# Moving convolution taps and softplus sums of a Mamba stage to GpSimd, and z's gate off it

## The reference, cut to what matters

```
xz = h @ W_in;  xm, z = split(xz, 2)
xm = silu(depthwise_conv4(xm) + conv_b)
dtr, Bm, Cm = split(xm @ W_xp, [64, 80])
dt = softplus(dtr @ W_dt + b_dt)
for each step t:  h = h * exp(dt_t * A) + (dt_t * x_t) * B_t
                  y_t = sum over states of h * C_t
y = (y + xm * D_param) * silu(z)
out = y @ W_out
```

## Time and profile before

| what | value |
|---|---|
| median of three runs | 2338.74 us |
| the profiled execution: its time, its span | 2343.22 us, 2341.5 us |
| busy: TensorE, VectorE, ScalarE, GpSimd | 2053.8, 2057.8, 1682.8, 1345.3 us |
| mean granted TensorE clock | 0.968 of full speed |
| scan from its first to its last bank product | 610.49 to 2273.23 us |

### The profile page before, as it was taken

One profiled execution on the slowest core, in us unless ns is written; L12 is line 12 of the kernel. 1 busy time (PEld: TensorE's weight loads), 2 busy tenths in 40 slices (PEclk: granted clock), 3 DMA queues, 4 the chain that ended last, 5 costly groups with the idle time before them and its releaser, 6 DMA issues. The chain is left out here.

```text
span 2341.5 us, 44346 instructions
## 1 busy us (share of the span) xinstructions
PE 2053.8 (88%) x13497; PEld 1578.5 (67%) x13497; DVE 2057.8 (88%) x3846; ACT 1682.8 (72%) x3652; POOL 1345.3 (57%) x1544
## 2 busy tenths in 40 slices
PE   4899999995799999999999999999999999989870
PEld 3566666662576767777777768777776768777760
DVE  2788888884599999999999999999999999999983
ACT  1455555553788979888888879888887879888840
POOL 2799999984455646455455646455455646454530
PEclk8999999996799999999999999999999999999995
DMA  5122222211000000000000000000000000000218
GB/s 142 39 64 64 64 64 64 62 47 34 10 6 14 6 14 15 6 15 6 19 6 14 6 15 15 6 15 5 20 6 15 5 15 15 6 6 6 90 73 287
DMA packets 71470, 80.75 MB, mean 34 GB/s; under 512 B 12227, under 2 KB 63619, under 8 KB 69188
## 3 DMA queue, kind: packets, MB, share of 16 engines
q1 hardware_dynamic: 66052, 69.52, 9.2%
q10 hardware_dynamic: 5184, 8.39, 1.0%
HBM read 44.33 MB, written 33.55 MB: 33 GB/s over the span
## 5 line engine op out<-in xcount | busy, mean ns | idle before, releaser
L599 ACT ACTIVATE decay<-dtT,decay_rate 128x256 f32<-128x256 f32 x2048 | 869.4, 495 | 0.2
L495 PE MATMUL bank<-ident,decay 128*128 128x128 f32 x4096 | 623.0, 275 | 114.1 <-DVE fresh L715 39.4
L505 PEld LDWEIGHTS bank<-ident,scaled 128*128 128x128 f32 x4096 | 485.5, 142 | 233.2 <-issue 201.9
L505 PE MATMUL bank<-ident,scaled 128*128 128x128 f32 x4096 | 623.7, 275 | 2.1 <-POOL scaled L446 2.0
L495 PEld LDWEIGHTS bank<-ident,decay 128*128 128x128 f32 x4096 | 470.9, 141 | 159.4 <-ACT decay L599 127.1
L446 POOL TENSOR_SCALAR scaled<-state,bc 128x512 f32<-128x512 f32 x384 | 276.8, 728 | 432.0 <-DVE state L715 402.7
L446 POOL TENSOR_SCALAR scaled<-fresh,bc 128x512 f32<-128x512 f32 x384 | 283.8, 747 | 317.8 <-DVE fresh L715 260.6
L705 DVE TENSOR_TENSOR bank<-bank,fresh 128x512 f32<-128x512 f32 x512 | 338.7, 689 | 58.2 <-PE bank L495 56.2
L705 DVE TENSOR_TENSOR bank<-bank,state 128x512 f32<-128x512 f32 x512 | 334.6, 688 | 28.6 <-PE bank L495 22.9
L715 DVE SCALAR_TENSOR_TENSOR state<-dtx,bc,bank 128x512 f32<-128x512 f32 x512 | 356.5, 736 | 0.0
L715 DVE SCALAR_TENSOR_TENSOR fresh<-dtx,bc,bank 128x512 f32<-128x512 f32 x512 | 356.4, 735 | 0.0
(11 more groups left out here) (137 smaller groups left out, 3427.7 us busy)
## 6 DMA issues: line engine op xcount, KB each, us to landing
xt<-in_x_dram SPq DMA_DIRECT2D x64, 128.0 KB, 2.2
resid<-x SPq DMA_DIRECT2D x64, 128.0 KB, 1.8
normed<-xh SPq DMA_DIRECT2D x64, 128.0 KB, 1.7
xg<-normed SPq DMA_DIRECT2D x64, 128.0 KB, 2.1
ssm_out<-yo SPq DMA_DIRECT2D x32, 256.0 KB, 2.0
fin_r<-resid SPq DMA_DIRECT2D x8, 1024.0 KB, 13.1
mask_bc<-in_mask_BxS_ik_dram SPq DMA_DIRECT2D x64, 64.0 KB, 2.9
fin_y<-ssm_out SPq DMA_DIRECT2D x32, 128.0 KB, 3.0
```

What stands on the lines that cost most here:

```text
L495: mm = pe.transpose(dec_bank[i % DECAY_BANKS][:, m * P:(m + 1) * P], decay[:, i // BLOCK % 2, n % GROUP, m, t % HALF * P:(t % HALF + 1) * ...
L505: mm = pe.matmul(y_bank[t % HALF][:, m * P:(m + 1) * P], scaled[:, i % RING, m * P:(m + 1) * P], ident[:, :], is_transpose=True, start=Fal ...
L599: act.activation(decay[:, block % 2, e // CB, m, :], dtT[par][:, m, half * HTOK:(half + 1) * HTOK], ACT.Exp, scale=decay_rate[:, m, n:n + ...
```

## The change

Four parts move.

1. The taps of blocks 0 and 1 go to GpSimd. Each tap is there two instructions: a product of `raw` with the tap into the new tile `tap`, and a sum of `tap` into `xs` (`add_tap`, items 6 to 17, one instruction an item). VectorE keeps the six taps of blocks 2 and 3 (items 10 to 16). The blocks are gated in the order 0, 2, 3, 1 (`X_ORDER`), tanh at items 13, 16, 18, 20 and gate at items 15, 17, 19, 21.
2. The softplus sum goes to GpSimd: for each block a sum and then the product with x, eight instructions at items 39 to 46 (`softplus_times_x`). ScalarE's first dt instruction becomes Relu in place of Identity, so that the sum has no maximum in it.
3. z is no longer copied: ScalarE takes its tanh straight from the bank, and VectorE makes (tanh + 1) * z with z read from the bank (items 17, 18, 22, 30), which also frees the bank. The tanh over all of z and GpSimd's eight gate instructions go.
4. The order of the jobs: z3 stands between dt0 and dt1, at items 28 and 29; z2 moves to 20 and 21; dt1 to dt3 stand at 31, 33, 35, bc at 36 to 39, x0 to x3 at 49, 51, 53, 55. dtr takes the blocks in the order of `X_ORDER`.

Waits follow: ScalarE's absolute value of dt waits for all four gated blocks (`tmp` is used for both), the carry copy waits for both kinds of taps, VectorE's first y gate waits for the four z banks, and the last prefetch of the sync engine waits for x3 of chunk 14 in place of z.

```diff
-        JOBS = ("h0 h1 u0 u1 u2 u3 out1 z0 z1 z2 z3 "
-                "dtr dt0 dt1 dt2 dt3 bc out0 x0 x1 x2 x3").split()
+        JOBS = ("h0 h1 u0 u1 u2 u3 out1 z0 z1 z2 "
+                "dtr dt0 z3 dt1 dt2 dt3 bc out0 x0 x1 x2 x3").split()
...
-                                (14, 15), (16, 17), (18, 19), (20, 21),
-                                (22, 23, 24, 25), (27,), (29,), (31,), (33,), (35, 36, 37, 38),
-                                (42, 43, 44), (46,), (48,), (50,), (52,))))
...
+                                (14, 15), (16, 17), (20, 21),
+                                (22, 23, 24, 25), (27,), (28, 29), (31,), (33,), (35,), (36, 37, 38, 39),
+                                (42, 43, 44), (49,), (51,), (53,), (55,))))
+        POOL_TAPS = [(m, k) for m in (0, 1) for k in range(TAPS - 1)]
+        POOL_TAP_SLOT = 6
+        VECTOR_TAPS = {10: (2, 0), 12: (2, 1), 14: (2, 2), 13: (3, 0), 15: (3, 1), 16: (3, 2)}
+        X_ORDER, X_TANH, X_GATE = (0, 2, 3, 1), (13, 16, 18, 20), (15, 17, 19, 21)
+        Z_GATE = (17, 18, 22, 30)
+        MODULATE, CARRY, SOFTPLUS = (28, 33), 24, 39
...
+            def add_tap(c, par, at, step):
+                m, k = POOL_TAPS[at]
+                done = (c + 1) * len(POOL_TAPS) + at
+                x = xs[1 - par][:, m, :]
+                if step == 0:
+                    if k == 0:
+                        gp.wait_ge(s_tap0, (c + 1) * CB + m + 1)
+                    reached(gp, s_tapadd, done)
+                    apart(gp)
+                    gp.tensor_scalar(tap[:, :], raw[:, m, k * P:k * P + TOK], taps[:, m, k:k + 1], 1.0,
+                                     ALU.mult, ALU.mult).then_inc(s_tapmul, 1)
+                else:
+                    gp.wait_ge(s_tapmul, done + 1)
+                    gp.tensor_tensor(x, x, tap[:, :], ALU.add).then_inc(s_tapadd, 1)
+            def softplus_times_x(c, par, m, step):
+                v = dtT[1 - par][:, m, :]
+                if step == 0:
+                    gp.wait_ge(s_softexp, (c + 2) * (CB + 1))
+                    gp.tensor_tensor(v, v, tmp[:, m, :], ALU.add).then_inc(s_dt, 1)
+                else:
+                    gp.wait_ge(s_dt, (c + 1) * CB + m + 1)
+                    gp.tensor_tensor(tmp[:, m, :], v, xs[1 - par][:, m, :], ALU.mult).then_inc(s_dtxT, 1)
...
-                    ins = act.activation(zs[1 - par][:, k, :], side[:, :], ACT.Copy)
+                    act.activation(zs[1 - par][:, k, :], side[:, :], ACT.Tanh, scale=0.5).then_inc(s_ztanh, 1)
+                    return
...
+                            ve.scalar_tensor_tensor(z, z, 1.0, side_bank[b][:, :], ALU.add, ALU.mult)\
+                                .then_inc(s_side_moved[b], 1)
```

More of the change, by code:

```diff
@@ L161, in build @@
         bc = sb("bc", [P, 2, T, 2 * DS], ssm_mem)
+        tap = sb("tap", [P, TOK], ssm_mem)
         decay = sb("decay", [P, 2, GROUP, CB, HTOK], ssm_mem)
@@ L244, in build @@
         s_gated = sem("y_gated")
-        s_zmul = sem("z_times_tanh")
         s_yo = sem("y_rows_ready")
@@ L451, in body @@
                         scale_state(c, par, i)
+                    if pre and 0 <= i - POOL_TAP_SLOT < 2 * len(POOL_TAPS):
+                        add_tap(c, par, (i - POOL_TAP_SLOT) // 2, (i - POOL_TAP_SLOT) % 2)
                     if pre and i in MODULATE and c + 2 < CHUNKS:
@@ L459, in body @@
                             .then_inc(s_carried, 1)
[L460 to L476, removed]
+                    if pre and SOFTPLUS <= i < SOFTPLUS + 2 * CB:
+                        softplus_times_x(c, par, (i - SOFTPLUS) // 2, (i - SOFTPLUS) % 2)
             modulate(0, 0)
@@ L620, in move @@
                 elif kind == "dt":
-                    act.activation(dtT[1 - par][:, k, :], side[:, :], ACT.Identity, bias=dt_bias[:, k:k + 1])
-                    act.wait_ge(s_xs, (c + 1) * CB + k + 1)
+                    act.activation(dtT[1 - par][:, k, :], side[:, :], ACT.Relu, bias=dt_bias[:, k:k + 1])
+                    act.wait_ge(s_xs, (c + 2) * CB)
                     ins = act.activation(tmp[:, k, :], side[:, :], ACT.Abs, bias=dt_bias[:, k:k + 1])
@@ L658, in body @@
                             move(c, par, job)
[L659 to L663, removed]
+                    if pre and i in X_TANH:
+                        m = X_ORDER[X_TANH.index(i)]
+                        last = (m, TAPS - 2)
+                        if last in POOL_TAPS:
+                            act.wait_ge(s_tapadd, (c + 1) * len(POOL_TAPS) + POOL_TAPS.index(last) + 1)
+                        else:
+                            act.wait_ge(s_tap, (c + 1) * len(VECTOR_TAP_ORDER) + VECTOR_TAP_ORDER.index(last) + 1)
                         act.activation(tmp[:, m, :], xs[1 - par][:, m, :], ACT.Tanh, scale=0.5).then_inc(s_xtanh, 1)
@@ L720, in gate @@
                 if t == 0:
-                    ve.wait_ge(s_zs, (c + 1) * CB)
+                    for k in range(CB):
+                        moved(ve, c - 1, f"z{k}")
                 ve.wait_ge(s_summed, c * ITEMS + index_of(DS - 1, t) + 1)
@@ L762, in body @@
                                                     ALU.mult, ALU.add).then_inc(s_tap, 1)
[L763 to L774 removed]
+                        if pre and s in Z_GATE:
+                            k = Z_GATE.index(s)
+                            ve.wait_ge(s_ztanh, (c + 1) * CB + k + 1)
+                            b = side_turn(c, f"z{k}")[0]
+                            z = zs[1 - par][:, k, :]
+                            ve.scalar_tensor_tensor(z, z, 1.0, side_bank[b][:, :], ALU.add, ALU.mult)\
+                                .then_inc(s_side_moved[b], 1)
+                        if pre and s in X_GATE:
+                            m = X_ORDER[X_GATE.index(s)]
+                            ve.wait_ge(s_xtanh, (c + 1) * CB + X_GATE.index(s) + 1)
+                            ve.scalar_tensor_tensor(xs[1 - par][:, m, :], tmp[:, m, :], 1.0, xs[1 - par][:, m, :],
+                                                    ALU.add, ALU.mult).then_inc(s_xs, 1)
             mamba_bodies(ve, body)
```

37 lines of the change are left out of this document (14 added, 23 removed).

## The result

| | before | after |
|---|---|---|
| median, four runs each | 2338.91 us | 2361.61 us (2360.53 to 2364.41) |
| profiled execution: time, span | 2343.22, 2341.5 | 2364.41, 2362.7 |
| one chunk of the scan, most of them | 105.15 | 105.52 |
| end of the state's clearing to the scan's first item | 52.97 | 61.74 |

After to before is 1.0079, with a 95% interval of [1.0065, 1.0094]: 0.8% slower, which is small but clear of the noise. The forecast was 2350, range 2325 to 2370.

What follows compares the result with a forecast made beforehand. VectorE, TensorE and ScalarE were taken to bound different stretches of a chunk. 15 x (0.05 + 0.55) + 2.5 = 11.5 on the profiled 2343.2 gave 2354.7; with the median 4.5 lower, 2350 us, range 2325 to 2370.

Steps and rivals of the forecast that it cites:

- meetings: Items 8 to 20: VectorE instructions with two SBUF operands slowed beside GpSimd's, 2.37 us a chunk in all.
- Item 8 to item 20: VectorE's time over these items of a chunk, pairs, taps, gates, output rows and waits summed: 27.85 us.
- Item 22's transpose: TensorE's transpose issued at item 22: saved taps eaten by waits and z gates, so 0.05 us later.
- the large meeting: Item 14: VectorE's second tap held behind GpSimd's sum of block 1, 1.10 us.
- z3's copy was ahead of the chain ... Item 43's transpose comes 0.55 later: Items 22 to 48: z3's tanh lengthens ScalarE's dt and decay chain, delaying TensorE's transpose 0.55 us a chunk.
- Softplus: nothing gained, nothing lost in the loop: Before item 43: taking the 2.61 us sum off VectorE gains nothing, since item 43 waits for its transpose anyway.
- Sum +2.5 (0 to +6): Body(-1), where nothing hides anything: its delays and savings together add 2.5 us, bounds 0 to 6.
- block 1's sum and dtr: Body(-1): block 1's tap sum on GpSimd is ready about 1.3 us later.
- A: Rival: VectorE is the bound throughout, a chunk saves 4.8 us, 2269 us in all; chance 0.05.
- D: Rival: two more meetings with a sum, +2.0 us a chunk, 2380 us in all; chance 0.13.
- B: Rival: GpSimd and VectorE phases miss each other, item 22 is 1.0 to 1.6 us earlier, 2326 us; chance 0.22.
- C: Rival: no change, since z3's tanh finds a gap in ScalarE's work, 2342 us; chance 0.23.

Runs made afterwards that it cites:

- e4: Changed kernel without GpSimd's twelve tap instructions: 2341.32 us, 0.9986 of the kernel before; chunk 104.50 us.
- e1: Kernel before with only the taps of blocks 0 and 1 moved to GpSimd and the new block order: 2335.15 us, 0.9955 of the kernel before.
- e2: Kernel before with only the z part and the new job order, taps and softplus left on VectorE: 2383.49 us, 1.016 of the kernel before.
- e5: Changed kernel without ScalarE's tanh of z3, all products and bank waits kept: 2361.91 us, 1.0077 of the kernel before.
- e9: Changed kernel with z3's product moved behind dt3, to items 34 and 35: 2358.03 us, 1.0067 of the kernel before.
- e6: Changed kernel with the old places of z2, z3, dt1 to dt3 and bc: 2356.2 us, 1.0055 of the kernel before.
- e3: Kernel before with only the softplus sum moved to GpSimd, Relu for Identity and later x jobs: 2344.45 us, 0.9999 of the kernel before.
- e11: Kernel before with taps of blocks 0 and 1 on GpSimd except in body(-1), and out0 at items 54, 57, 60: 2289.84 us, 0.9773.
- e7: Changed kernel with all of body(-1)'s taps on VectorE: 2362.04 us, 1.0081 of the kernel before.

## Why the prediction was right, and where it was not

The direction and the reason for it were right: VectorE gave up 62.7 us (I had said 50 to 70), and the loop did not get shorter: up to item 20 the saved taps went into waits for TensorE, meetings and z gates, and before item 43 ScalarE is last. The kernel is 22.7 us slower by medians; I said 11.3. Step by step:

- **Item 8 to item 20: 27.85 forecast, 27.20 measured.** The waits for TensorE are 2.3 for 2.46 (0.35, 1.84 and 0.13 by starts), the meetings 1.9 for 2.37 (0.15, 0.58, 1.02, 0.15), the two z gates 1.20 for 1.31. Every term is there and each a little too large. How much a meeting costs of the time that GpSimd's instruction has left was an estimate of mine; what was measured of it stands at the end of this section. Item 22's transpose came 0.48 earlier, not 0.05 later. That the large meeting, 1.02, counts in full is shown by e4; that the taps by themselves are a gain and the gates take it back is shown by e1 and e2: at item 20, 37.51 without the gates and 38.69 with them.
- **"z3's copy was ahead of the chain ... Item 43's transpose comes 0.55 later": the failed step.** From item 22's transpose to item 43's it is 0.82 more: the size was near, the cause was wrong. I added the tanh (0.5) to ScalarE's chain and took it that z3's product on TensorE was covered by the waits for ScalarE. It is not: dt1's product now stands 3.5 us further behind dt0's, and the chain becomes 23.49 for 22.68, with the tanh (e5: nothing moves without it) or without. With the product out of the way (e9) the term that I had is what is left, 0.47. With z3 ahead of the chain (e6) all 0.81 are gone.
- **Softplus: nothing gained, nothing lost in the loop.** Right, e3.
- **"Sum +2.5 (0 to +6)" for body(-1): mis-sized, +8.8.** Three of its terms hold: dt chain +1.15 for 0.9, GpSimd's eight instructions +2.83 for 3.4, tanh and gates at the end -2.56 for -3.2. The fourth does not: block 1's sum and dtr are 7.35 late, not 1.3. GpSimd's twelve instructions are one after another on the path. Its first two pairs take 2.26 each, six such 13.4; together they take 16.0. I put 1.3 for this. e1, which has no z gate, has 6.12 of the 7.35: most of it is the taps. I also forgot that z2's bank is now given back by VectorE's gate, behind the taps, where before ScalarE's copy did it; that was to be seen in the diff. It makes a wait of 5.72, but most of that lies beside the taps, and what it adds to e1's 6.12, the clock's fall included, is 1.2. In the whole front the taps alone cost 7.1 (e1), the z part alone 0.8 (e2), and with neither on the path the front is 54.4 (e11). The parts don't add.
- **Not foreseen: the clock.** Two chunks lose 1.2 to 1.3 us each, and chunk 0 grew by 1.3 more than the others; its first 6.5 us are at half clock (before 4.9), but no run shows that this is the cause. Why chunks 5 and 9 and not their neighbours, with the same gap, stays open.

In sum the loop came to 15 x 0.37 = 5.5, 2.8 for chunks 5 and 9, 1.3 for chunk 0, less 0.6 for a chunk of before that was long by itself: 9.1 where I had 9.0 (15 x 0.60). That agreement is luck, since I had none of the last three terms. Body(-1) was 6.3 more than I had; 3.3 is the clearing and the tail; and the median of after lies 2.8 under its profiled execution, not the 4.5 that I took over from before. These make 11.4 of the 11.6 between 2350 and 2361.6.

The rivals: A (VectorE the bound throughout) and D (two more meetings with a sum) did not happen. Nor did B (the meetings miss each other): e1's chunk gained 1.26, near B's 1.0, but with every meeting in place (2.43 for the two taps at item 14), so the size is B's and the reason is not. What e1 lacks is the two z gates, 1.20. C's condition did come true, z3's tanh found a gap (e5), and still its time did not: the gap is itself made by z3's product.

What two of the meetings of chunk 8 cost of the time that GpSimd's instruction had left: the tap that started at 1486.72 began 0.36 before GpSimd's scaling ended (1486.38 + 0.70) and lost 0.15 to it. The meeting with the sum cost 1.02: the second tap began at 1496.18, and the sum had 1.21 left. In both the loss was smaller than what was left, by 0.21 and 0.19.

## What to carry to other kernels

Read which engine is last stretch by stretch before pricing an edit: VectorE's 62.7 us brought nothing, since they went into waits for TensorE and ScalarE and into meetings and gates, while moving sixteen matmuls a chunk out of a full stretch into one with gaps, with no work saved, gave 1.5%. When work moves onto an engine that is idle in the loop, price it also where nothing runs beside it: twelve GpSimd instructions cost 7 us once, in front (e1). When the reader of a bank moves from one engine to another, look for what stands ahead of it on the new engine: the bank comes back that much later. And test the parts of a change one by one: here one part was a gain, one was nothing and one a loss larger than both.

## What the runs showed of the hardware

- A gap of 2.48 to 2.58 us in TensorE's work ahead of item 22, in a loop where it is busy 98.15 of 105.52 us (chunk 8 of the kernel after), came in some chunks with 3.4 us at half clock (of chunks 1 to 14, 2 in the kernel after, 3 in e5 and in e7, 8 in e2, 7 in e9), each 1.2 to 1.4 us of time. Where the longest gap at that place was 1.47 (e4), 1.25 (e6) or 0.18 (e1), there was no fall in these chunks.
- VectorE operations with two SBUF operands took longer where GpSimd had begun one before them: taps of 0.75 took 0.89 beside a scaling and up to 1.77 beside a sum, x gates of 0.68 up to 2.8 (e7) beside an operation of 128x1024. The z gate, one operand of which is in a bank, took 0.67 to 0.69 in all its 64 executions, also beside the sum of 578.95 (0.68 from 579.32 on). GpSimd's own instructions took longer too beside VectorE's taps and x gates: products 1.12 and up to 1.42 for 0.69, sums up to 1.68 for 1.28. The source view of the kernel after, durations in ns, least, median and most:

```profile
L781 DVE SCALAR_TENSOR_TENSOR xs<-raw,taps,xs x96: 751/891/1767, 570.7 to 2135.7; 128x512 f32<-128x512 f32 x96
```
